# One transformer block in fp32 precision on one core: the values of steps 0 and 1, 2 and 3, 4 and 5, 6 and 7 taken together, the next input's transposes ahead of the last first-layer slice, and the first layer's banks dealt out anew

## The chip, the core and the metric
The kernel runs on one of the eight cores of a Trainium2 chip. The time is that of the device, in microseconds (us). The engines of the core are TensorE (PE, with its weight loads as PEld), VectorE (DVE), ScalarE (ACT), GpSimd (POOL) and SyncE (SP, which issues the DMAs). Each runs its own program in order, and semaphores join them.

## The reference
There are 32 inputs of 512 tokens by 256 features. Each goes through attention and a feed-forward part, both with a residual:
```
x = x + attention(layernorm(x))
x = x + 0.5 * (silu(layernorm'(x) @ w1 + b1) @ w2 + b2)
```
The attention is linear, with 16 heads of 16 features, q and k through elu(x)+1, and causal in chunks of 128 tokens. For each chunk (n = 4 of them) and head:
```
scores = mask(q k^T);  num = scores v + q S;  den = sum(q * (cumsum(k) + z))
out = num / den;  S += k^T v;  z += sum(k)
```
The first layer w1 is 256 by 1024, the second w2 1024 by 256, both dequantised from integers. layernorm' has a gain and an offset.

## The kernel before
The work is a software pipeline over the 32 inputs. One pass of the loop, called a **slice** here, does the attention of input i, the feed-forward part of input i-1 and the projection of q and k of input i+1. Slice 0 has no feed-forward part; slices 1 to 29 are the loop, 30 and 31 are written out with parts left away, and slice 32 has the feed-forward part alone. The order on each engine is written out by hand: `pe_iteration` for PE, `ve_iteration` for DVE, `ac_iteration` for ACT, `po_iteration` for POOL.

The attention of a slice has eight **steps** u = 0..7 (two halves t of the heads, four chunks c). For each step:
- `scores(u)`: PE, 4 matmuls of 128 by 256 into two PSUM banks (L454);
- `mask(u)`: DVE, two multiplications by the causal mask, from the two banks into the buffer `probs[u % 2]` (L624, 128x512 each);
- `values(u)`: PE, 8 matmuls of 32 columns of weights into `num[t]`, 16 records in the trace (L496). It waits for both masks of the step;
- `from_state(u)`: PE, the part from the running state, one matmul, two records (L463); none for chunk 0.

When a head half is done, `attention(t)` on DVE multiplies `num[t]` by the reciprocal denominators (L743). These were transposed by PE in `spread_reciprocals(t)` (L528) and copied by ACT in `reciprocals_out(t)` (L975).

Between the steps PE does the first layer in eight pieces `fc1(j)`, each 4 matmuls of 128x512 into two banks a and b (L390, L391). ACT scales bank a (`ffn_scaled`, L889), DVE adds bank b (`ffn_sum`, L710), ACT takes silu and makes the high part (`ffn_silu`, L897 and L900), POOL makes the low part (L1028). High and low parts exist because every matmul of full precision is made as three.

`x_transposes` (L358) turns the next input over. ACT copies the high part `xt_hi` (L878) and DVE makes the low part `xt_lo` (`input_lo`, L654), one for each half t. `project_kq(0)` and `project_kq(1)` are 12 matmuls of 128x512 each (L328). Then come the second layer `fc2`, the output projection, and, at the slice's end, the values projection, the transposes of the feed-forward input and `scores(0)` of the next slice.

PSUM has 8 banks: `num0`, `num1`, `state_acc`, `sc0`, `sc1` and three of a ring. The table `RING` says which ring bank a use takes, in order of time, and `free_bank` makes a use wait for the last read of the use before it in the same bank. Uses in `BORROWED` take other banks, with waits of their own.

Of the kernel before, what the change touches and what calls it, by code (L numbers as in the profile page):

```python
# [73 lines left out]
def build(nc, x, wq_t, bq, wk_t, bk, wv_t, bv, wo_t, bo, gamma, beta, q1, sc1, b1, q2, sc2, b2, out):  # L74
# [20 lines left out]
    with ExitStack() as ctx:  # L95
# [66 lines left out]
        def by_group(ap):  # L162
# [11 lines left out]
        ring = [bank(f"ring{n}") for n in range(3)]  # L174
        RING = {"ht0": 0, "v1": 2, "kt1": 1, "f1a": 0, "f1b": 2, "f2a": 1, "f2b": 0, "f3a": 2, "f3b": 1, "rb0": 0,
                "f4a": 2, "f4b": 0, "f5a": 1, "f5b": 2, "rb1": 0, "f6a": 1, "f6b": 0, "f7a": 2, "f7b": 1,
                "xt0": 0, "xt1": 2, "k0": 0, "q0": 1, "z0": 0, "wo0": 2, "z1": 1}
        USES = list(RING)
        NEXT_USES = {"xt0", "xt1", "k0", "q0"}

        BORROWED = {"v0": state_acc, "kt0": state_acc, "ht1": num[0], "f0a": num[0], "f0b": num[1], "wo1": num[0]}
        FFN_USES = {"ht0", "ht1", "z0", "z1"} | {f"f{j}{ab}" for j in range(FT) for ab in "ab"}
# [100 lines left out]
        def free_bank(w, use, present):  # L283
# [13 lines left out]
            if use == "f0b":  # L297
                if "rb0" in present:
                    w.need(rden, 0)
                else:  # L300
                    w.need(attn, -1, 1)
                return
            if use == "wo1":
                w.need(attn, 0, 0)
                return
            n = USES.index(use)
# [54 lines left out]
        def pe_iteration(e, i, A, Fn, N, N2, preparation=None, bias_products=None, first=False):  # L361
# [195 lines left out]
            if not A and Fn:  # L557
                fc1(2)
                for j in range(FT):
                    if j + 3 < FT:  # L560
                        fc1(j + 3)
                    fc2_group(j)
                return
            fc1(2)
            if A:
                scores(1)
                update_states()
                values(0)
            for u in range(2, U, 2):
                if u < U - 2:  # L570
                    fc1(2 * (u // 2) + 1)
                if u == U - 2:
                    fc1(FT - 1)
                if A and u < U - 2:
                    spread_reciprocals(u // 2 - 1)
                if A:
                    scores(u)
                if u < U - 2:
                    fc1(2 * (u // 2) + 2)
                elif N:  # L580
                    x_transposes()
                if A:
                    scores(u + 1)
                    values(u - 1)
                    values(u)
                    from_state(u - 1)
                    from_state(u)
            if preparation:
                preparation()
            project_kq(0)  # L590
            if A:
                values(U - 1)
                from_state(U - 1)
            project_kq(1)
# [61 lines left out]
        def ve_iteration(e, i, A, Fn, N, N2, preparation=(None, None, None)):  # L656
# [137 lines left out]
            if A:  # L794
                snapshots(0)
                snapshots(1)
                mask(2)
            ffn_sum(3)
            ffn_sum(4)
            if A:  # L800
                mask(3)
                mask(4)
            ffn_sum(5)
            ffn_sum(6)
            if A:
                mask(5)
                mask(6)
                attention(0)
            ffn_sum(7)
            input_lo()  # L810
            if A:
# [61 lines left out]
        def ac_iteration(e, i, A, Fn, N, N2, preparation=None):  # L873
# [102 lines left out]

            for j in range(3, FT - 1):
                ffn_scaled(j)
                if j in (3, 5):
                    reciprocals_out((j - 3) // 2)  # L980
                ffn_silu(j - 1)
            ffn_scaled(FT - 1)
            if N:
                for t in range(T):
                    w.need(v_pe, 0)
                    transposed_hi(f"xt{t}", t, xt_pe, xt_hi, 1, xt_h)
            def attention_hi(t):
                if A:
# [344 lines left out]
```

How the kernel before makes its waits and increments, by code:

```python
    def need(self, event, shift=0, k=None):  # L63
        k = event.per - 1 if k is None else k
        if self.known.get((id(event), shift), -1) >= k:
            return
        self.known[(id(event), shift)] = k
        value = event.value(self.i + shift, k)
        if not isinstance(value, int) or value > 0:
            self.engine.wait_ge(event.sem, value)
# [1060 lines left out]
        @block.sync  # L1132
        def _(e):
            e.dma_start(x_in[:, :, :], x_v[0]).then_inc(load.sem, 16)
            src = {"q": wq_t, "k": wk_t, "v": wv_t, "o": wo_t}
            for n in WORDER:
                e.dma_start(stage_of(n), src[n].rearrange("(t p) n -> p t n", p=P)).then_inc(p_wdma[n], 16)
            e.dma_start(bias_o[:, :], on_all(bo)).then_inc(p_dma, 16)
            for t in range(T):
                e.dma_start(w1_i[t], q1[t * P:(t + 1) * P, :]).then_inc(p_wdma["1"], 16)
            early(e, store)
            e.wait_ge(p_const, CONSTS - 1)
            e.wait_ge(p_zero, 1)
            sp_iteration(e, -1, False, False, True, True, lambda: e.wait_ge(p_v, V_W1))
            for n in range(2):
# [10 lines left out]
            with e.Fori(1, B - 2) as i:  # L1157
                sp_iteration(e, i, True, True, True, True)
            sp_iteration(e, B - 2, True, True, True, False)
            sp_iteration(e, B - 1, True, True, False, False)
            sp_iteration(e, B, False, True, False, False)
            e.wait_ge(store.sem, store.value(B - 1, 1))
```

## Time and profile before
| | us |
|---|---|
| median of three runs | 1546.86 (1544.33 to 1548.13) |
| the profiled execution, whole | 1547.17 |
| its span in the trace | 1545.3 |
| PE busy | 1500.6 (97%) |
| DVE busy | 1285.4 (83%) |
| ACT busy | 1131.0 (73%) |
| POOL busy | 671.1 (43%) |

PE's matmuls are pipelined: their lengths overlap in the trace. What one costs is therefore read as the distance from its start to the start of the next. The same holds in part for DVE and ACT, where the next instruction starts before the last has ended.

### The profile page before, as it was taken

The page shows a single profiled execution, that of the slowest core. Times are in us where ns is not written, and L with a number is a line of the kernel's source. Part 1 is how long each engine was busy: PE and PEld are TensorE (multiplying, and loading weights), DVE is VectorE, ACT ScalarE, POOL GpSimd, SP SyncE. Part 2 cuts the span into 40 slices and gives each one's busy share as a digit, 9 for nine tenths or more (in the row PEclk, how much of TensorE's full clock was granted, in tenths as well). Part 3 has the DMA queues.
Part 4 walks back from the last instruction along what each step waited for, and adds up shares of the span by engine and source line. Part 5 has one row for each costly group of instructions (what it writes and reads, how often), then busy time and mean ns, then how long its engine had stood idle before and what let it go on. Part 6 is the DMA issues. An engine that isn't in the chain of part 4 may idle for free.

```text
span 1545.3 us, 40671 instructions
## 1 busy us (share of the span) xinstructions
PE 1500.6 (97%) x14820; PEld 1307.8 (85%) x14820; DVE 1285.4 (83%) x2587; ACT 1131.0 (73%) x1917; POOL 671.1 (43%) x466
## 2 busy tenths in 40 slices
PE   5799999999999999999999999999999999999997
PEld 5588888888888888888888888888888888888887
DVE  6888888888888888888888888888888888888865
ACT  4487777787777787777787777787777787777763
POOL 3245344544344544344544344544344444344443
PEclk8899999999999999999999999999999999999999
DMA  7946775555775555775556775556775556765540
GB/s 197 218 104 130 176 175 134 138 126 133 176 176 124 140 131 135 176 176 123 123 145 138 176 163 139 132 130 141 176 166 129 127 138 146 176 173 124 112 97 28
DMA packets 153944, 222.96 MB, mean 144 GB/s; under 512 B 20032, under 2 KB 71488, under 8 KB 153920
## 3 DMA queue, kind: packets, MB, share of 16 engines
q1 hardware_dynamic: 152560, 222.63, 60.6%
q8 instruction: 15, 0.25, 0.1%
q10 hardware_dynamic: 1360, 0.01, 0.1%
q14 instruction: 9, 0.07, 0.0%
HBM read 138.69 MB, written 83.89 MB: 144 GB/s over the span
## 4 chain that ended last, share of the span: by engine, by line
PE 89%; DVE 6%; issue 3%; DMA 1%; ACT 0%; SPq 0%; DVEq 0%; POOL 0%; ACTq 0%
PE ring L328 35%; PE ring L390 7%; PE ring L391 7%; PE num L496 6%; PE sc L454 6%; PE sc L328 5%; PE num L463 3%; PE num L328 3%; PE state_acc L328 3%; PE ring L528 2%; PE state_acc L477 2%; PE state_acc L454 1%; DVE xt_lo L654 1%; DVE qk L743 1%; DVE probs L624 1%
## 5 line engine op out<-in xcount | busy, mean ns | idle before, releaser
L1028 POOL TENSOR_TENSOR s_lo<-silu_f,s_hi 128x512 fp32r<-128x512 f32 x256 | 342.9, 1345 | 498.3 <-ACT s_hi L900 498.2
L624 DVE TENSOR_TENSOR probs<-sc,causal 128x512 f32<-128x512 f32 x416 | 271.5, 685 | 71.8 <-PE sc L454 62.0
L328 PE MATMUL ring<-w_hi,s_hi 128*128 128x256 f32 x992 | 282.7, 285 | 1.8 <-issue 1.8
L328 PE MATMUL ring<-w_lo,s_hi 128*128 128x256 f32 x992 | 279.4, 282 | 0.0
L328 PE MATMUL ring<-w_hi,s_lo 128*128 128x256 f32 x992 | 279.3, 282 | 0.0
L328 PEld LDWEIGHTS ring<-w_hi,s_hi 128*128 128x128 f32 x992 | 187.9, 189 | 15.7 <-issue 14.4
L1044 POOL TENSOR_TENSOR qk<-qk,phi_q 128x512 f32<-128x512 f32 x64 | 82.9, 1296 | 262.6 <-DVE qk L677 262.6
L328 PEld LDWEIGHTS ring<-w_lo,s_hi 128*128 128x128 f32 x992 | 188.2, 190 | 1.3
L328 PEld LDWEIGHTS ring<-w_hi,s_lo 128*128 128x128 f32 x992 | 188.0, 190 | 0.0
L390 PE MATMUL ring<-gt_hi,w_q 128*128 128x512 f32 x441 | 187.4, 425 | 0.0
L889 ACT ACTIVATE silu_f<-ring,bias,scale 128x512 f32<-128x512 f32 x217 | 167.4, 771 | 14.1 <-PE ring L391 11.5
L391 PE MATMUL ring<-gt_lo,w_q 128*128 128x512 f32 x441 | 174.2, 395 | 0.0
L710 DVE SCALAR_TENSOR_TENSOR silu_f<-ring,scale,silu_f 128x512 f32<-128x512 f32 x222 | 165.6, 746 | 10.2 <-ACT silu_f L889 1.4
L1012 ACT ACTIVATE den_rows<-num 128x256 f32<-128x256 f32 x32 | 12.3, 385 | 219.2 <-PE num L511 219.2
L897 ACT ACTIVATE silu_f<-silu_f 128x512 f32<-128x512 f32 x256 | 159.7, 624 | 13.0 <-DVE silu_f L710 9.3
L900 ACT ACTIVATE s_hi<-silu_f 128x512 fp32r<-128x512 f32 x256 | 161.9, 633 | 8.1
L454 PE MATMUL sc<-q_stack,k_stack 96*128 96x256 f32 x832 | 153.8, 298 | 3.5 <-DVE probs L624 2.0
L496 PE MATMUL num<-probs,v_pad 128*32 128x128 f32 x4096 | 145.1, 276 | 1.7 <-DVE probs L624 1.0
L454 PEld LDWEIGHTS sc<-q_stack,k_stack 96*128 96x128 f32 x832 | 121.8, 191 | 19.3 <-DVE probs L624 11.4
L496 PEld LDWEIGHTS num<-probs,v_pad 128*32 128x32 f32 x4096 | 102.7, 110 | 26.6 <-issue 12.3
L390 PEld LDWEIGHTS ring<-gt_hi,w_q 128*128 128x128 f32 x441 | 82.9, 188 | 37.6 <-ACT silu_f L889 11.4
L391 PEld LDWEIGHTS ring<-gt_lo,w_q 128*128 128x128 f32 x441 | 83.4, 189 | 8.8
(189 smaller groups left out, 3816.2 us busy)
## 6 DMA issues: line engine op xcount, KB each, us to landing
k_stack<-k_rows SPq DMA_DIRECT2D x192, 256.0 KB, 4.0
q_stack<-q_rows SPq DMA_DIRECT2D x384, 128.0 KB, 6.3
k_rows<-silu_f SPq DMA_DIRECT2D x128, 256.0 KB, 3.8
q_rows<-probs SPq DMA_DIRECT2D x128, 256.0 KB, 4.1
x_in<-in_x SPq DMA_DIRECT2D x32, 512.0 KB, 8.6
xb<-in_x SPq DMA_DIRECT2D x32, 512.0 KB, 8.3
out<-clip SPq DMA_DIRECT2D x64, 256.0 KB, 7.8
silu_f<-in_q SPq DMA_DIRECT2D x2, 512.0 KB, 10.7
```

Of the source, the lines that this page charges most:

```text
L328: last = e.matmul(target, a, b, start=(n == 0), stop=(n == 3 * len(pairs) - 1))
L390: e.matmul(bank_[:, :], w1_q[:, t, cols], gt_hi[:, t, :], start=True, stop=False)
L391: f_pe.done(e.matmul(bank_[:, :], w1_q[:, t, cols], gt_lo[:, t, :], start=False, stop=True))
L454: last = e.matmul(score_bank(u, r)[:, 2 * n * P:2 * (n + 1) * P], k_stack[:, t, pair, toks], q_stack[:, t, pair, :, toks], start=True, sto ...
L496: last = e.matmul(num[t][32 * pair:32 * pair + 32, c * P:(c + 1) * P], v_pad[:, c, t * HT // 2 + pair, 2 * odd:2 * odd + 2, :], probs[u % ...
L624: masked[r].done(e.tensor_tensor(half_probs(u, r), score_bank(u, r)[:, :].rearrange("p (h q) -> p h q", h=HV), causal[:, None, :].to_broad ...
L710: f_b.done(e.scalar_tensor_tensor(out=slot, in0=ffn_bank(j, 1, A)[:, :], scalar=scale_1[:, 1, j:j + 1], in1=slot, op0=ALU.mult, op1=ALU.add))
L889: f_a.done(e.activation(silu_f[:, j % SLOTS, :], ring_bank(f"f{j}a")[:, :], ACT.Identity, bias=bias_1[:, j:j + 1], scale=scale_1[:, 0, j:j ...
L897: silu.done(e.activation(slot, slot, ACT.Silu))
L900: sh.done(e.activation(s_hi[:, j, :], slot, ACT.Copy))
L1028: sl.done(e.tensor_tensor(s_lo[:, j, :], silu_f[:, j % SLOTS, :], s_hi[:, j, :].bitcast(F32), ALU.subtract))
L1044: qkcum.done(e.tensor_tensor(qk[:, t, :], qk[:, t, :], phi_q[:, t, :], ALU.mult))
```

## The change
On PE, `scores(1)` goes ahead of `fc1(2)`. The values go in pairs (0,1), (2,3), (4,5), (6,7); before they went 0, (1,2), (3,4), (5,6), 7. `x_transposes` goes ahead of `fc1(7)`, and `values(6)` follows `project_kq(0)` together with `values(7)`. On DVE, `mask(3)` goes ahead of `ffn_sum(3)`, `mask(5)` ahead of `ffn_sum(5)`, `attention(0)` stands between `mask(4)` and `mask(5)`, and `input_lo` ahead of `ffn_sum(7)`. On ACT, the copies `xt_hi` go ahead of `ffn_silu(5)` and `ffn_scaled(7)`. The ring's banks are dealt out anew; `f7b` borrows `num0`.

```diff
--- before.py
+++ after.py
@@ -172,13 +172,13 @@
         state_acc = bank("state_acc")
         sc = [bank(f"sc{r}") for r in range(2)]
         ring = [bank(f"ring{n}") for n in range(3)]
-        RING = {"ht0": 0, "v1": 2, "kt1": 1, "f1a": 0, "f1b": 2, "f2a": 1, "f2b": 0, "f3a": 2, "f3b": 1, "rb0": 0,
-                "f4a": 2, "f4b": 0, "f5a": 1, "f5b": 2, "rb1": 0, "f6a": 1, "f6b": 0, "f7a": 2, "f7b": 1,
-                "xt0": 0, "xt1": 2, "k0": 0, "q0": 1, "z0": 0, "wo0": 2, "z1": 1}
+        RING = {"ht0": 0, "v1": 2, "kt1": 1, "f1a": 0, "f1b": 2, "f2a": 1, "f2b": 0, "rb0": 2, "f3a": 1, "f3b": 0,
+                "f4a": 2, "f4b": 1, "rb1": 0, "f5a": 2, "f5b": 1, "f6a": 0, "f6b": 2, "xt0": 1, "xt1": 0, "f7a": 2,
+                "k0": 0, "q0": 1, "z0": 0, "wo0": 2, "z1": 1}
         USES = list(RING)
         NEXT_USES = {"xt0", "xt1", "k0", "q0"}
 
-        BORROWED = {"v0": state_acc, "kt0": state_acc, "ht1": num[0], "f0a": num[0], "f0b": num[1], "wo1": num[0]}
+        BORROWED = {"v0": state_acc, "kt0": state_acc, "ht1": num[0], "f0a": num[0], "f0b": num[1], "f7b": num[0], "wo1": num[0]}
         FFN_USES = {"ht0", "ht1", "z0", "z1"} | {f"f{j}{ab}" for j in range(FT) for ab in "ab"}
 
         SCORES = {(0, 0): 0, (0, 1): 1, (1, 0): 0, (1, 1): 1, (2, 0): 0, (2, 1): 1, (3, 0): 0, (3, 1): 2,
@@ -300,8 +300,13 @@
                 else:
                     w.need(attn, -1, 1)
                 return
+            if use == "f7b":
+                if "rb0" in present:
+                    w.need(attn, 0, 0)
+                return
             if use == "wo1":
                 w.need(attn, 0, 0)
+                w.need(f_b, -1)
                 return
             n = USES.index(use)
             m = n - 1
@@ -561,35 +566,42 @@
                         fc1(j + 3)
                     fc2_group(j)
                 return
+            if A:
+                scores(1)
             fc1(2)
             if A:
-                scores(1)
                 update_states()
                 values(0)
-            for u in range(2, U, 2):
-                if u < U - 2:
-                    fc1(2 * (u // 2) + 1)
-                if u == U - 2:
-                    fc1(FT - 1)
-                if A and u < U - 2:
-                    spread_reciprocals(u // 2 - 1)
+                values(1)
+                spread_reciprocals(0)
+            for u in range(2, U - 2, 2):
                 if A:
                     scores(u)
-                if u < U - 2:
-                    fc1(2 * (u // 2) + 2)
-                elif N:
-                    x_transposes()
+                fc1(u + 1)
                 if A:
                     scores(u + 1)
-                    values(u - 1)
+                fc1(u + 2)
+                if A:
                     values(u)
-                    from_state(u - 1)
-                    from_state(u)
+                    values(u + 1)
+                    for step in range(u - 1 if u == 2 else u, u + 2):
+                        from_state(step)
+                    if u == 2:
+                        spread_reciprocals(1)
+            if A:
+                scores(U - 2)
+            if N:
+                x_transposes()
+            fc1(FT - 1)
+            if A:
+                scores(U - 1)
             if preparation:
                 preparation()
             project_kq(0)
             if A:
+                values(U - 2)
                 values(U - 1)
+                from_state(U - 2)
                 from_state(U - 1)
             project_kq(1)
             if bias_products:
@@ -795,19 +807,19 @@
                 snapshots(0)
                 snapshots(1)
                 mask(2)
+                mask(3)
             ffn_sum(3)
             ffn_sum(4)
             if A:
-                mask(3)
                 mask(4)
+                attention(0)
+                mask(5)
             ffn_sum(5)
             ffn_sum(6)
             if A:
-                mask(5)
                 mask(6)
-                attention(0)
+            input_lo()
             ffn_sum(7)
-            input_lo()
             if A:
                 mask(7)
             if A:
@@ -974,16 +986,21 @@
                     w.need(rb_pe, 0, t)
                     rb_sb.done(e.activation(qk[:, t, :], ring_bank(f"rb{t}")[:, :], ACT.Copy))
 
-            for j in range(3, FT - 1):
-                ffn_scaled(j)
-                if j in (3, 5):
-                    reciprocals_out((j - 3) // 2)
-                ffn_silu(j - 1)
-            ffn_scaled(FT - 1)
+            reciprocals_out(0)
+            ffn_scaled(3)
+            ffn_silu(2)
+            ffn_scaled(4)
+            ffn_silu(3)
+            reciprocals_out(1)
+            ffn_scaled(5)
+            ffn_silu(4)
+            ffn_scaled(6)
             if N:
                 for t in range(T):
                     w.need(v_pe, 0)
                     transposed_hi(f"xt{t}", t, xt_pe, xt_hi, 1, xt_h)
+            ffn_silu(5)
+            ffn_scaled(7)
             def attention_hi(t):
                 if A:
                     w.need(attn, 0, t)
```

In the pieces below, names with a number are PSUM banks or buffers, and the brackets name the semaphores that an instruction waits for. The first is PE's order in the loop at steps 4 and 5, before: scores(5), values(3) with values(4), from_state(3), fc1(6).
```order
L454 MATMUL state_acc<-q_stack,k_stack 128x256 [waits masked1]
L454 MATMUL state_acc<-q_stack,k_stack 128x256
L454 MATMUL sc1<-q_stack,k_stack 128x256 [waits masked0]
L454 MATMUL sc1<-q_stack,k_stack 128x256
L496 MATMUL num0<-probs1,v_pad 32x128 x8
L496 MATMUL num1<-probs0,v_pad 32x128 [waits masked1]
L496 MATMUL num1<-probs0,v_pad 32x128 x7
L463 MATMUL num0<-phi_q,k_tok 128x128
L390 MATMUL ring2<-gt_hi,w1_q 128x512 [waits f_b]
```
The same place of the changed kernel, from the second half of scores(5): fc1(6), values(4) with values(5), from_state(5).
```order
L459 MATMUL sc1<-q_stack,k_stack 128x256 [waits masked0]
L459 MATMUL sc1<-q_stack,k_stack 128x256
L395 MATMUL ring0<-gt_hi,w1_q 128x512 [waits rb_sb]
L396 MATMUL ring0<-gt_lo,w1_q 128x512
L71 REGISTER_ALU
L395 MATMUL ring2<-gt_hi,w1_q 128x512 [waits f_a]
L396 MATMUL ring2<-gt_lo,w1_q 128x512
L501 MATMUL num1<-probs0,v_pad 32x128 [waits masked1]
L501 MATMUL num1<-probs0,v_pad 32x128 x7
L501 MATMUL num1<-probs1,v_pad 32x128 [waits masked1,masked0]
L501 MATMUL num1<-probs1,v_pad 32x128 x7
L468 MATMUL num1<-phi_q,k_tok 128x128
```
Values(5), which reads `probs1`, now follows values(4) directly; before, values(4) was the last there, and values(5) stood behind the scores of steps 6 and 7.

The second is PE's order in the loop ahead of the projection of q and k, before: the second half of the transposes, scores(7), values(5) with values(6), from_state, first matmul of the projection.
```order
L358 MATMUL ring2<-ident,x_hat 128x128 [waits f_a]
L358 MATMUL ring2<-ident,x_hat 128x128 x3
L454 MATMUL sc1<-q_stack,k_stack 128x256 [waits masked1]
L454 MATMUL sc1<-q_stack,k_stack 128x256
L454 MATMUL sc0<-q_stack,k_stack 128x256 [waits masked0]
L454 MATMUL sc0<-q_stack,k_stack 128x256
L496 MATMUL num1<-probs1,v_pad 32x128 x8
L496 MATMUL num1<-probs0,v_pad 32x128 [waits masked1]
L496 MATMUL num1<-probs0,v_pad 32x128 x7
L463 MATMUL num1<-phi_q,k_tok 128x128 x2
L71 ISA
L328 MATMUL ring0<-xt_hi,wk_hi 128x512 [waits xt_l]
```
The same place of the changed kernel: the second half of the transposes, fc1(7), scores(7), first matmul of the projection.
```order
L71 REGISTER_ALU
L363 MATMUL ring0<-ident,x_hat 128x128 [waits f_a]
L363 MATMUL ring0<-ident,x_hat 128x128 x3
L395 MATMUL ring2<-gt_hi,w1_q 128x512 [waits f_b]
L396 MATMUL ring2<-gt_lo,w1_q 128x512
L395 MATMUL num0<-gt_hi,w1_q 128x512 [waits attn]
L396 MATMUL num0<-gt_lo,w1_q 128x512
L459 MATMUL sc1<-q_stack,k_stack 128x256 x2
L459 MATMUL sc0<-q_stack,k_stack 128x256 [waits masked0]
L459 MATMUL sc0<-q_stack,k_stack 128x256
L71 ISA
L333 MATMUL ring0<-xt_hi,wk_hi 128x512 [waits xt_l]
```
Before, the first half of the transposes went to `ring0` and the second to `ring2`; now the first goes to `ring1` (just above the piece) and the second to `ring0`, where the projection of k starts. Values and from_state no longer stand ahead of the projection.

The third is DVE's order in the loop at steps 4 and 5, before.
```order
L624 TENSOR_TENSOR probs0<-sc1,causal 128x512 [waits av_pe,sc_pe]
L624 TENSOR_TENSOR probs0<-sc0,causal 128x512
L71 REGISTER_ALU
L71 REGISTER_ALU [waits f_a]
L710 SCALAR_TENSOR_TENSOR silu_f<-ring2,scale_1,silu_f 128x512 [waits f_pe]
L71 REGISTER_ALU
L71 REGISTER_ALU [waits f_a]
L710 SCALAR_TENSOR_TENSOR silu_f<-ring0,scale_1,silu_f 128x512 [waits f_pe]
L624 TENSOR_TENSOR probs1<-state_acc,causal 128x512 [waits av_pe,sc_pe]
L624 TENSOR_TENSOR probs1<-sc1,causal 128x512
```
The same place of the changed kernel.
```order
L636 TENSOR_TENSOR probs0<-sc1,causal 128x512 [waits av_pe,sc_pe]
L636 TENSOR_TENSOR probs0<-sc0,causal 128x512
L755 TENSOR_TENSOR qk<-num0,qk 128x512 [waits num_pe,rb_sb]
L71 REGISTER_ALU
L636 TENSOR_TENSOR probs1<-state_acc,causal 128x512 [waits av_pe,sc_pe]
L636 TENSOR_TENSOR probs1<-sc1,causal 128x512
L71 REGISTER_ALU [waits f_a]
L722 SCALAR_TENSOR_TENSOR silu_f<-ring1,scale_1,silu_f 128x512 [waits f_pe]
L71 REGISTER_ALU
L71 REGISTER_ALU [waits f_a]
L722 SCALAR_TENSOR_TENSOR silu_f<-ring2,scale_1,silu_f 128x512 [waits f_pe]
```
Between the masks of step 4 and those of step 5 stand two `ffn_sum` (L710) before, and `attention(0)` (L755) now; the two sums follow the masks of step 5.

## Rows read from the trace of the kernel before
**Rows 1.** The page, parts 1 and 2: busy time of the engines, and the granted clock.
```profile
PE 1500.6 (97%) x14820; PEld 1307.8 (85%) x14820; DVE 1285.4 (83%) x2587; ACT 1131.0 (73%) x1917; POOL 671.1 (43%) x466
...
PEclk8899999999999999999999999999999999999999
```

**Rows 2.** Chain of waits, longest pieces: start us, length us, what; second layer.
```profile
108.64 7.12 PE ring L328 x60
...
1455.89 7.12 PE ring L328 x60
```

**Rows 3.** Timeline of PE, one slice: start us, length us, instruction.
```profile
409.86 0.50 PE L390 MATMUL ring<-gt_hi,w_q 128*128 128x512 f32 x1
410.20 0.40 PE L391 MATMUL ring<-gt_lo,w_q 128*128 128x512 f32 x1
...
414.21 0.39 PE L390 MATMUL ring<-gt_hi,w_q 128*128 128x512 f32 x1
...
415.16 0.50 PE L454 MATMUL sc<-q_stack,k_stack 96*128 96x256 f32 x2
...
415.82 1.08 PE L496 MATMUL num<-probs,v_pad 128*32 128x128 f32 x32
416.83 0.71 PE L463 MATMUL num<-phi_q,k_tok 128*128 128x128 f32 x4
417.30 0.48 PE L390 MATMUL ring<-gt_hi,w_q 128*128 128x512 f32 x1
417.62 0.40 PE L391 MATMUL ring<-gt_lo,w_q 128*128 128x512 f32 x1
...
423.01 0.40 PE L454 MATMUL sc<-q_stack,k_stack 96*128 96x256 f32 x2
...
423.49 1.04 PE L358 MATMUL ring<-ident,x_hat 128*128 128x128 f32 x8
424.29 0.72 PE L454 MATMUL sc<-q_stack,k_stack 96*128 96x256 f32 x4
...
425.95 0.71 PE L463 MATMUL num<-phi_q,k_tok 128*128 128x128 f32 x4
426.89 0.50 PE L328 MATMUL ring<-xt_hi,wk_hi 128*128 128x512 f32 x1 [0.23 <-DVE xt_lo L654]
...
429.89 0.64 PE L496 MATMUL num<-probs,v_pad 128*32 128x128 f32 x16
430.46 0.49 PE L463 MATMUL num<-phi_q,k_tok 128*128 128x128 f32 x2
...
433.60 0.28 PE L328 MATMUL ring<-w_hi,s_hi 128*128 128x256 f32 x1
```

**Rows 4.** Timeline of DVE, the same slice; idle time and its releaser in brackets.
```profile
419.43 1.29 DVE L624 TENSOR_TENSOR probs<-sc,causal 128x512 f32<-128x512 f32 x2 [0.98 <-PE sc L454]
...
423.69 0.69 DVE L624 TENSOR_TENSOR probs<-sc,causal 128x512 f32<-128x512 f32 x1 [0.22 <-PE state_acc L454]
424.30 0.68 DVE L624 TENSOR_TENSOR probs<-state_acc,causal 128x512 f32<-128x512 f32 x1
...
426.15 1.28 DVE L654 TENSOR_TENSOR xt_lo<-ring,xt_hi 128x512 fp32r<-128x512 f32 x2
...
431.48 0.75 DVE L666 SCALAR_TENSOR_TENSOR phi_k<-ring,bias_qk,clip 128x512 f32<-128x512 f32 x1 [2.05 <-ACT clip L927]
```

**Rows 5.** Timeline of ACT, the same slice.
```profile
425.69 0.63 ACT L991 ACTIVATE gt_hi<-qk 128x512 fp32r<-128x512 f32 x1 [0.47 <-DVE qk L743]
426.23 0.61 ACT L897 ACTIVATE silu_f<-silu_f 128x512 f32<-128x512 f32 x1
...
427.41 0.62 ACT L897 ACTIVATE silu_f<-silu_f 128x512 f32<-128x512 f32 x1
```

**Rows 6.** Timeline of DVE in slice 0.
```profile
47.16 1.29 DVE L624 TENSOR_TENSOR probs<-sc,causal 128x512 f32<-128x512 f32 x2 [2.07 <-PE sc L454]
```

**Rows 7.** Busy time by stretch, slice 0: PE, PEld, DVE, ACT, POOL, clock, DMA.
```profile
45.00:50.00 5.00, 4.32 (x59) 3.44 (x54) 2.26 (x5) 0.60 (x1) 2.27 (x1) 1.00 1.07 340
```

## The prediction
> **What bounds the kernel now.** I read the page first: PE is busy for 97% of the span, DVE for 83%, ACT for 73%, at full clock but for the first two fortieths [rows 1]. So PE sets the time, and others matter only where PE waits for them. Next the length of a slice: the 60 second-layer matmuls start at 108.64 and, 29 slices later, at 1455.89 [rows 2]; that is 1347.25 / 29 = 46.46 us, and the loop's slices are alike. Then PE's timeline in one slice, start to start. A slice here is PE's work plus four small losses, and the change touches all of them.
>
> Unit costs on PE, each from start to start [rows 3]. Four first-layer matmuls: 414.21 to 415.16, 0.95 us. Four scores matmuls: 423.01 to 423.49, 0.48. The eight transposes: 423.49 to 424.29, 0.80; I add the 0.07 that the last of such matmuls leaves to the next group (as from_state does, below), 0.87. Values of two steps: 415.82 to 416.83, 1.01; of one step: 429.89 to 430.46, 0.57. So a second step joined to a first costs 0.44, and a block of values has 0.13 that it pays once.
>
> Unit costs on DVE and how fast a wait ends [rows 3, 4]. Masks start 0.60 apart (423.69, 424.30) and one lasts 0.68. The last of the four scores matmuls that start at 423.01 starts at 423.37 and lasts 0.28 (the length of the 256-column matmul at 433.60), so it ends at 423.65; its mask starts at 423.69, 0.04 later. The first `xt_lo` starts at 426.15, ends about 0.68 later at 426.83, and PE goes on at 426.89: 0.06 later. And a matmul that waited could not load its weights beforehand: 409.86 to 410.20 is 0.34 where a first-layer matmul takes 0.235, so each wait costs about 0.10 on top.
>
> **The change part by part, for one slice of the loop.**
>
> One block of values less. Before there are five blocks (0 is joined to the state update), now four. A block costs its 0.13; on entry, the four scores from 415.16 take 0.66 to 415.82 where 0.48 is their work and 0.10 the reload after a wait, so 0.08; on leaving, from_state of two steps takes 0.47 (416.83 to 417.30) and the first-layer matmul behind it 0.32 (to 417.62) where 0.235 is its work, so 0.09. Sum 0.30: gain 0.30. Bounds: 0.1 (only the part inside the block) to 0.4.
>
> fc1(2) no longer waits. It waits at 409.86 for ACT's copy of fc1(1)'s bank: about 0.10, and 0.10 reload. `scores(1)`, 0.48, now stands between. Gain 0.20; bounds 0.1 to 0.2.
>
> scores(3) keeps its wait. Its first bank must be masked for step 2, and fc1(3) alone lies between, as before. The 415.16 row is this wait: its two matmuls take 0.34 to the next rather than 0.24. Cost 0, bounds -0.1 to 0.1.
>
> values(3) waits now. It follows values(2), where before it stood a step later. Count from the start of the last scores(3) matmul. DVE: 0.28 + 0.04, one mask start 0.60, one mask 0.68, 0.05 to PE: 1.65. PE: 0.12 + fc1(4) 0.95 + entry 0.08 + values(2) 0.44 = 1.59. Wait 0.06, and about 0.04 for a load of only 32 columns: cost 0.10, bounds 0 to 0.2.
>
> values(5) waits now, and this is the largest new item. From the last scores(4) matmul, DVE does two masks, `attention(0)`, two masks: 0.28 + 0.04 + 4 x 0.60 + 0.68 + 0.05 = 3.45. DVE is free by then: it idles 0.98 ahead of these masks [rows 4], and has less to do there now. PE: 0.12 + fc1(5) 0.95 + scores(5) 0.48 + fc1(6) 0.95 + 0.08 + values(4) 0.44 = 3.02. Wait 0.43, with the load 0.47. Bounds 0.2 to 0.6. Behind the waiting instruction on PE stand scores(6), the transposes and the whole projection, so nothing hides it.
>
> The projection of k. Before: from_state at 425.95 would end its 0.47 at 426.42, and the projection starts at 426.89 [rows 3]; wait 0.47. This is what putting the transposes first should cure. But the second half of the transposes now goes to `ring0`, where the projection of k starts, so that the projection waits for both low parts rather than for one. From the last scores(6) matmul: 0.28 + 0.04, two masks and the first `xt_lo` 3 x 0.60, the second `xt_lo` 0.68, 0.05: 2.85, and the reload 0.10 makes 2.95. PE: 0.12 + transposes 0.87 + fc1(7) 0.95 + scores(7) 0.48 = 2.42. Wait 0.53 against 0.47: cost 0.06. Bounds -0.3 (the first low part were enough, 0.60 earlier, less what comes late elsewhere) to 0.2.
>
> fc2(0) may wait now. It takes `ring0` after `phi_k`. Between `xt_hi` and the exponentials ACT does one silu pair more (426.23 to 427.41, 1.18) and one scaling (about 0.7), and saves the 0.47 idle ahead of 425.69 [rows 5] and a little more: the exponentials come 1.3 later, and with them `phi_k`, which follows ACT directly (2.05 idle ahead of it [rows 4]). From the transposes' start, `phi_k` ended at 431.48 + 0.75 - 423.49 = 8.74, now 10.0. PE came to fc2(0) after 433.60 - 423.49 = 10.11, and now after 0.87 + 0.95 + 0.48 + 0.53 + 2.82 + (0.10 + 1.01 + 0.47 + 0.08) + 2.82 = 10.13. The margin is 0.1, of the size of the reload. I take 0.10, bounds 0 to 0.3.
>
> Per slice: -0.30 - 0.20 + 0.10 + 0.47 + 0.06 + 0.10 = +0.23. I round it to 0.2, since two of the terms are of the size of my reading. Slices 1 to 30: 30 x 0.2 = 6. Slice 31 has no next input: -0.5 + 0.57, about 0.1.
>
> **Slice 0** has no first layer on PE, so DVE and PE wait for each other there. Before, DVE still had the odd step's masks while PE did values; now each pair of steps is closed before the next begins. From the end of mask(3) to the start of mask(4), PE does values(3) 0.44 + 0.13, from_state(1, 2, 3) 0.7, four transposes 0.44, scores(4) 0.48 and some 0.4 of releases and leaving: 2.6; between mask(1) and mask(2) it is some 1.0 behind the state's snapshots, between mask(5) and mask(6) 0.57 + 0.24 + 0.48 + 0.4 = 1.7. DVE's idle time there is 2.07 ahead of 47.16 in the profile [rows 6], with about 1.6 at the other two places by the same counting, and DVE is busy for only 2.26 of the 5 us at 45 to 50 [rows 7]. That makes 5.3 against 3.7, 1.6 more; and the projection now follows mask(6) and both low parts (1.2 + 1.3 behind scores(6)) where it had been reached with them done: 1.4 more. Cost 3; bounds 0 (DMA or DVE hides it later) to 5 (PE is longer at the lower clock, of which the two 8s of [rows 1] tell).
>
> Sum: 6 + 0.1 + 3 = 9.1, against the profiled execution's own 1547.17 (span 1545.3 and 1.9 around it). It lies 0.3 over the median of the runs, within their spread. **Forecast: 1556.3 us.** Its own range by the bounds of the terms that matter: -0.05 to +0.45 a slice and 1 to 5 for slice 0, 1547 to 1566, and mostly 1551 to 1561.
>
> **The rivals.**
>
> *The gains win (faster).* If the wait at values(5) is covered, a slice is -0.24, and the whole 1547.2 - 7.2 + 3 = 1543. Place: PE's arrival at values(5). It decides at 0.23: with a wait there under that, a slice is shorter than before. For it: the gains of 0.30 and 0.20 are read from rows, and if leaving a block costs more than I can see they grow. Against: five DVE instructions of known length stand between scores(4) and values(5), and PE's work between is shorter by 0.4.
>
> *It cancels (no change).* A slice at 0 to +0.05 and slice 0 hidden behind its DMAs and DVE's preparation of the weights: 1547 to 1550. For it: the three small terms (values(3), projection, fc2(0)) sum to 0.26 and each could be nil. Against: slice 0's chain goes through DVE, which has no slack to hide it in.
>
> *ACT becomes late (slower still).* Its chain from the exponentials on is 1.3 later while PE is only 0.2 later. If the denominators or the next slice's inputs have under 1.1 of slack, up to 0.5 a slice more: 1556 + 15 = 1571.
>
> *The clock falls (slower still).* Three waits a slice instead of one large one. The clock stays at full in the loop although each slice has its 0.47 us wait [rows 1], which speaks against it. If PE did 1 us of each slice at 1.2 GHz, it would take 2: 1556 + 31 = 1587. The Trainium skill ("TensorE: Matmul & The Clock Gate", section A second HAM failure mode) says that a kernel whose PE idles briefly and often between groups of matmuls lost throughput to a clock that goes down and up; by that rule this rival would come true, and no row here shows it yet.
>
> **How the numbers follow.** Forecast 0.72, faster rival 0.10, cancelling 0.12, ACT late 0.04, clock 0.02. A measurement of this kernel tells about 0.3% (4.6 us) from no change. Below 1542.2 is faster: half of the faster rival and tails, 0.08. Slower, above 1551.5: nearly all of the forecast's own share and the two slower rivals, 0.76. The rest, 0.16, is no change. Range 1549 to 1563, which leaves out most of the faster rival and the slowest cases.
>
> **What would show it.** The slice by the distance between the second layers: 46.6 to 46.7 rather than 46.46. On PE, values of one step followed by an idle or stretched start (about 0.45) where values(5) starts, released by the mask; four blocks of values; no stretch at fc1(2) in its new place; 0.5 ahead of the projection, released by the second `xt_lo`. In slice 0, DVE idle 2.6 or more ahead of mask(4), and the first second layer 3 us later. It is wrong if the slice is under 46.5, or if PE comes to values(5) with both masks done.

## The result, and the profile after

| | before | after |
|---|---|---|
| time, median of 5 runs each | 1545.0 us | 1581.45 us (1580.27 to 1585.82) |
| ratio | | 1.0242, interval 1.0228 to 1.0256 |
| span of the profiled execution | 1545.3 us | 1578.5 us |
| one slice of the loop | 46.46 us | 47.42 us |

The change costs 2.4%, four times the 9 us that were forecast; 1563 was the end of the range. Two executions among the experiments below, far slower than the others of their kernel (1619.05 and 3652.11 us), count in no median or ratio. The page, parts 1 and 2, as [rows 1] of before:
```profile
PE 1514.8 (96%) x14820; PEld 1302.0 (82%) x14820; DVE 1325.2 (84%) x2587; ACT 1125.2 (71%) x1917; POOL 670.6 (42%) x466
...
PEclk8899999999999999999999999999999999999999
```
The clock is as before. DVE has the same 2587 instructions and is busy for 39.8 us more: some of them last longer, namely two kinds of subtraction that make low parts, `silu_f<-phi_k,silu_f` (70.7 us in all before, 89.2 after) and `gt_lo<-qk,gt_hi` (49.9 and 73.6). The chain of waits gives the slice, as [rows 2]:
```profile
114.35 7.12 PE ring L333 x60
...
1489.41 7.25 PE ring L333 x60
```
(1489.41 - 114.35) / 29 = 47.42. So 0.96 a slice was added, where 0.2 was forecast. The list of waits of after (what PE waited with, its line, the releaser; then us in total, times, longest) says where:
```profile
PE num L501 <- DVE probs L636: 14.2, 34, 1.4
PE ring L333 <- DVE xt_lo L666: 11.6, 32, 2.0
...
PE ring L363 <- ACT x_hat L957: 7.8, 31, 3.0
```
The first is mainly values(5), the second the projection; both were forecast. The third wasn't: in the kernel before PE waited for ACT's `x_hat` once in the whole run, for 2.4 us; now in every slice. `x_hat` (the program's name for the normalised input of the feed-forward, `hn2`) is what the first-layer transposes read at the end of a slice.

PE's timeline of one slice of after. A slice is measured here from its feature transposes (`state_acc<-ident,phi_k`):
```profile
418.99 0.60 PE L438 MATMUL state_acc<-ident,phi_k 128*128 128x128 f32 x4
...
428.55 1.25 PE L501 MATMUL num<-probs,v_pad 128*32 128x128 f32 x32
429.73 0.94 PE L468 MATMUL num<-phi_q,k_tok 128*128 128x128 f32 x6
...
433.85 0.64 PE L501 MATMUL num<-probs,v_pad 128*32 128x128 f32 x16
434.84 0.65 PE L501 MATMUL num<-probs,v_pad 128*32 128x128 f32 x16 [0.35 <-DVE probs L636]
435.41 0.49 PE L468 MATMUL num<-phi_q,k_tok 128*128 128x128 f32 x2
...
438.02 0.64 PE L459 MATMUL sc<-q_stack,k_stack 96*128 96x256 f32 x4
...
438.96 0.50 PE L333 MATMUL ring<-xt_hi,wk_hi 128*128 128x512 f32 x1 [0.29 <-DVE xt_lo L666]
...
446.31 0.34 PE L333 MATMUL ring<-w_hi,s_hi 128*128 128x256 f32 x1
446.50 0.28 PE L333 MATMUL ring<-w_lo,s_hi 128*128 128x256 f32 x1
...
461.38 0.38 PE L525 MATMUL num<-ident,den_rows 128*128 128x128 f32 x2
463.03 0.72 PE L363 MATMUL ring<-ident,x_hat 128*128 128x128 f32 x3
463.91 0.33 PE L363 MATMUL ring<-ident,x_hat 128*128 128x128 f32 x1 [0.16 <-ACT x_hat L957]
464.07 0.60 PE L363 MATMUL num<-ident,x_hat 128*128 128x128 f32 x4
...
466.42 0.60 PE L438 MATMUL state_acc<-ident,phi_k 128*128 128x128 f32 x4
```
The other engines in the same slice of after (ACT, DVE, POOL):
```profile
436.86 1.09 ACT L890 ACTIVATE xt_hi<-ring 128x512 fp32r<-128x512 f32 x2 [2.15 <-PE ring L363]
444.10 0.67 ACT L936 ACTIVATE clip<-ring,bias_qkm 128x512 f32<-128x512 f32 x1
461.77 2.08 ACT L957 ACTIVATE x_hat<-x,hn_add,ln_rstd 128x256 f32<-128x256 f32 x4 [1.31 <-DVE hn_add L874]
441.77 1.64 DVE L666 TENSOR_TENSOR gt_lo<-qk,gt_hi 128x512 fp32r<-128x512 f32 x1
447.39 1.36 DVE L701 TENSOR_TENSOR silu_f<-phi_k,silu_f 128x512 fp32r<-128x512 f32 x1
456.10 0.66 DVE L854 TENSOR_TENSOR x<-ring,xb 128x512 f32<-128x512 f32 x1
439.19 1.30 POOL L1045 TENSOR_TENSOR s_lo<-silu_f,s_hi 128x512 fp32r<-128x512 f32 x1 [3.80 <-ACT s_hi L912]
440.46 2.40 POOL L1052 TENSOR_TENSOR xb<-xb,bias_o 128x1024 f32<-128x1024 f32 x1
442.82 2.99 POOL L1045 TENSOR_TENSOR s_lo<-silu_f,s_hi 128x512 fp32r<-128x512 f32 x2
445.76 2.44 POOL L1056 TENSOR_TENSOR res<-res,bias 128x1024 f32<-128x1024 f32 x1
```
And the rows of before that answer to them, beyond [rows 3 to 5] (the next slice's feature transposes start at 453.00, so this one's at 453.00 - 46.46 = 406.54):
```profile
430.12 0.67 ACT L924 ACTIVATE clip<-ring,bias_qkm 128x512 f32<-128x512 f32 x1
447.60 2.07 ACT L945 ACTIVATE x_hat<-x,hn_add,ln_rstd 128x256 f32<-128x256 f32 x4
433.41 0.68 DVE L689 TENSOR_TENSOR silu_f<-phi_k,silu_f 128x512 fp32r<-128x512 f32 x1
437.97 1.53 DVE L689 TENSOR_TENSOR silu_f<-phi_k,silu_f 128x512 fp32r<-128x512 f32 x1
441.76 0.66 DVE L842 TENSOR_TENSOR x<-ring,xb 128x512 f32<-128x512 f32 x1
430.54 2.41 POOL L1039 TENSOR_TENSOR res<-res,bias 128x1024 f32<-128x1024 f32 x1
437.66 1.29 POOL L1044 TENSOR_TENSOR qk<-qk,phi_q 128x512 f32<-128x512 f32 x1 [4.71 <-DVE qk L677]
448.57 0.38 PE L520 MATMUL num<-ident,den_rows 128*128 128x128 f32 x2
450.22 0.60 PE L358 MATMUL ring<-ident,x_hat 128*128 128x128 f32 x4
450.65 0.60 PE L358 MATMUL num<-ident,x_hat 128*128 128x128 f32 x4
453.00 0.60 PE L433 MATMUL state_acc<-ident,phi_k 128*128 128x128 f32 x4
```
Subtract the slice's start from each and compare:

| from the slice's start, us | before | after | later by |
|---|---|---|---|
| ACT, first exponential (`clip<-ring`) | 23.58 | 25.11 | 1.53 |
| PE, fc2(0) | 27.06 | 27.32 | 0.26 |
| DVE, `x` (the attention's output added) | 35.22 | 37.11 | 1.89 |
| ACT, the four `x_hat`, start | 41.06 | 42.78 | 1.72 |
| PE, transposes of the denominators | 42.03 | 42.39 | 0.36 |
| PE, the transposes of `x_hat` into `num`, behind the wait | 44.11 | 45.08 | 0.97 |

Up to fc2(0) PE is 0.26 later; the forecast had 0.13 ahead of fc2(0) and 0.10 at it. At the denominators it is 0.36 later, where 0.23 was forecast. What follows, 0.97 - 0.36 = 0.61, is the wait for `x_hat`, of which the forecast had nothing. The last `x_hat` of before is ready at 447.60 + 2.07 = 449.67; the fourth transpose needs it some 0.33 behind 450.22, at 450.55. That is 0.88 of slack, the time by which an input is ready before PE reads it. Against PE, `x_hat` came 1.72 - 0.36 = 1.36 later, and PE now waits: its four transposes stretch from 0.43 to 1.04.

### The profile page after: what moved, and what is told of

The parts are those of the page before. It is cut to its first block, busy times and chain, and to the rows that moved or that the text cites. A ratio compares the mean times of both kernels' runs of the same rounds, so it can differ in the third digit from the quotient of the medians.

```text
span 1578.5 us, 40769 instructions
## 1 busy us (share of the span) xinstructions
PE 1514.8 (96%) x14820; PEld 1302.0 (82%) x14820; DVE 1325.2 (84%) x2587; ACT 1125.2 (71%) x1917; POOL 670.6 (42%) x466
## 4 chain that ended last, share of the span: by engine, by line
PE 65%; DVE 23%; issue 6%; ACT 4%; DMA 1%; DVEq 0%; SPq 0%; POOL 0%; ACTq 0%
PE ring L333 24%; PE num L501 8%; DVE probs L636 5%; PE sc L333 5%; PE sc L459 5%; PE num L468 4%; PE ring L395 4%; PE ring L396 4%; ACT x_hat L957 3%; DVE stats L859 3%; DVE stats L645 2%; DVE x L854 2%; DVE xt_lo L666 2%; DVE qk L689 2%; PE ring L533 2%
## 5 line engine op out<-in xcount | busy, mean ns | idle before, releaser
L501 PE MATMUL num<-probs,v_pad 128*32 128x128 f32 x4096 | 154.1, 278 | 14.3 <-DVE probs L636 14.2
L395 PE MATMUL ring<-gt_hi,w_q 128*128 128x512 f32 x410 | 164.9, 402 | 0.0
L396 PE MATMUL ring<-gt_lo,w_q 128*128 128x512 f32 x410 | 161.7, 394 | 0.0
L501 PEld LDWEIGHTS num<-probs,v_pad 128*32 128x32 f32 x4096 | 101.9, 110 | 67.5 <-issue 47.5
L722 DVE SCALAR_TENSOR_TENSOR silu_f<-ring,scale,silu_f 128x512 f32<-128x512 f32 x191 | 137.0, 743 | 5.4
L957 ACT ACTIVATE x_hat<-x,hn_add,ln_rstd 128x256 f32<-128x256 f32 x128 | 66.5, 590 | 56.2 <-DVE hn_add L874 56.2
L701 DVE TENSOR_TENSOR silu_f<-phi_k,silu_f 128x512 fp32r<-128x512 f32 x64 | 89.2, 1394 | 0.0
```

The costliest lines, as they stand in the source:

```text
L395: e.matmul(bank_[:, :], w1_q[:, t, cols], gt_hi[:, t, :], start=True, stop=False)
L396: f_pe.done(e.matmul(bank_[:, :], w1_q[:, t, cols], gt_lo[:, t, :], start=False, stop=True))
L501: last = e.matmul(num[t][32 * pair:32 * pair + 32, c * P:(c + 1) * P], v_pad[:, c, t * HT // 2 + pair, 2 * odd:2 * odd + 2, :], probs[u % ...
L722: f_b.done(e.scalar_tensor_tensor(out=slot, in0=ffn_bank(j, 1, A)[:, :], scalar=scale_1[:, 1, j:j + 1], in1=slot, op0=ALU.mult, op1=ALU.add))
L957: e_hn2.done(e.activation(hn2[:, c, :], x1[:, c, :], ACT.Identity, bias=hn2_add[:, c:c + 1], scale=ln2_rstd[:, 1, c:c + 1]))
```

## The experiments

The theory (A): ACT does the inputs' copies `xt_hi` ahead of the silu of block 5, stands idle for them (2.15 at 436.86), and all its later work in the slice is late by 1.53. In addition GpSimd's add of bias_2 now collides with DVE's subtraction for the low part of phi_k (they overlap in time, and the subtraction lasts 1.36 instead of 0.68). Both run down one chain: exponentials, DVE's features, `x`, statistics, GpSimd's rsqrt, ACT's `x_hat`. Rivals: PE's own new waits are dearer than they look; slice 0; the removed waits come back. Ratios are to the kernel before, run beside it. The slice is taken each time from the second layers in the chain of waits, as above.

**One ACT step back.**
```
 ffn_scaled(6)
+ffn_silu(5)
 if N: ... transposed_hi(...)      # xt_hi
-ffn_silu(5)
 ffn_scaled(7)
```


> The changed kernel, with one pair of ACT moved back: the silu of slice 5 and its high part ahead of the copies of the transposed input, in the time in which ACT idles for the transposes. Theory A (late chain): the changed kernel loses most of its time because ACT reaches the exponentials 1.53 us later in each slice; DVE's features, layer-norm statistics and the normalised input of the feed-forward part follow, and PE waits about 0.75 us for the latter ahead of its transposes at the slice's end. Then this edit takes about 1.2 us off the delay, PE's wait there and the one at the first second-layer matmul go, the slice falls from 47.41 to about 46.6 and the time from 1581 to 1556 (1550 to 1562). Theory B (PE's own waits at values(5), the projection and the pairs were mis-sized, and the late chain is covered): the slice stays over 47.1 and the time over 1572. Theory C (collisions of DVE and POOL alone): the time falls by under 15 us and the 1.35 us subtraction for the low part of k stays.

Measured: 1560.74 us, ratio 1.0096 (1.0073 to 1.0120); slice 46.73. One instruction pair's place on ACT gives back 21 of the 36 us. The wait for `x_hat` falls to 2 times a run, and the subtractions for phi_k's low part are again as before (mean 1104 ns against 1394 in after). What remains, 0.27 a slice, is PE's own part, close to the 0.23 that the prediction had summed for it.

**The add of bias_2 earlier on GpSimd**, ahead of its low part of block 4 (ACT still late).
```
 for j in range(2, FT):
+    if Fn and j == 4: res += bias_2
     ...
     ffn_lo(j)
-if Fn: res += bias_2
```


> The changed kernel, with POOL's addition of the bias to the residual (2.4 us) moved ahead of the fifth low part of the feed-forward, out of the stretch in which DVE subtracts the high part of k. Theory C (a part of the loss is a collision: DVE's first subtraction for the low part of k takes 1.35 us beside this addition, 0.68 in the kernel before): the subtraction falls to 0.7, the features of the second half are no longer 0.33 further behind, PE's wait at the slice's end falls by about 0.33, the time by about 10 us to 1571. Theory A without C: the length of that subtraction does not come from POOL, nothing moves, 1581. Both allow that the addition itself delays POOL's low parts by 2.4 us without anyone waiting.

Measured: 1571.04 us, 1.0161 (1.0137 to 1.0185); slice 47.09. DVE's subtraction lasts 0.69 again, though the exponentials are as late as in after; `x` comes 1.55 later than before, not 1.89. So about 0.33 a slice of the loss (47.42 - 47.09) is the collision. PE still waits for `x_hat`, 14 times in the list (5.0 us): here the lateness alone overruns the slack.

**DVE's attention(0) behind mask(5).**
```
 mask(4)
-attention(0)
 mask(5)
+attention(0)
```


> The changed kernel, with attention(0) on DVE behind mask(5) rather than ahead of it. Forecast by my own term: the wait of PE at values(5) falls from 0.45 to about 0.05, which is about 0.4 a slice. Theory A: the end of the slice is set by the chain through ACT and DVE, which is not a bit shorter except where it starts from PE (the transposes come up to 0.4 earlier, so ACT's copies do too): the time falls by up to 0.35 x 31, to about 1571, if the chain moves with PE, and not at all if ACT is bound by itself. Theory B: it falls by 0.4 x 31 = 12 us or more, to 1569 or less.

Measured: 1568.68 us, 1.0145 (1.0116 to 1.0173); slice 47.04. PE's waits for masks at L501 fall from 14.2 us (34) to 2.6 (3); those for `xt_lo` grow from 11.6 to 14.4; those for `x_hat` stay (7.9). PE comes to the transposes sooner, so ACT's copies and exponentials come 0.38 sooner too, which is what the slice gains. The time lies just within B's range, but the interval (1564 to 1573 us) covers both theories; what speaks for A is that the waits for `x_hat` stay and that the exponentials move by as much as the slice.

**The late ACT step put into the kernel before.** Nothing else is changed.
```
 ffn_scaled(6)
-ffn_silu(5)
 ffn_scaled(7)
 if N: ... transposed_hi(...)      # xt_hi
+ffn_silu(5)
```


> The kernel before, with nothing changed but ACT: the copies of the transposed input ahead of the silu of slice 5 (one pair, 1.2 us of which ACT had idled about half). Theory A: ACT reaches the exponentials about 0.7 us later; the fourth normalised chunk of the feed-forward input had about 0.75 of slack, so that PE waits 0 to 0.3 at the slice's end, more if DVE's subtraction now meets POOL: the time rises by 0 to 10 us. With PE's order untouched every rise is the late chain's. Theory B: no rise.

Measured: 1568.73 us, 1.0150 (1.0128 to 1.0173): +23 us, more than was expected. Slice 47.13. ACT's exponentials are only 0.57 later, but DVE's subtraction and GpSimd's add stand so:
```profile
439.87 2.00 DVE L689 TENSOR_TENSOR silu_f<-phi_k,silu_f 128x512 fp32r<-128x512 f32 x1
...
438.91 2.40 POOL L1041 TENSOR_TENSOR res<-res,bias 128x1024 f32<-128x1024 f32 x1
...
454.89 2.08 ACT L945 ACTIVATE x_hat<-x,hn_add,ln_rstd 128x256 f32<-128x256 f32 x4 [1.36 <-DVE hn_add L862]
```
2.00 where it was 0.68, and the slack of 0.88 is overrun: PE waits for `x_hat` 40 times, 8.7 us. A step moved on ACT reproduces two thirds of the loss with PE's order untouched. Is it the lateness or the collision?

**The same with the add of bias_2 early**, by the second experiment's edit.


> The kernel before with two edits: ACT copies the transposed inputs ahead of the silu of block 5 (the edit of the earlier run that cost 23 us), and GpSimd adds bias_2 to res ahead of its fourth low part instead of behind its last. In that earlier run the exponentials came 0.58 us later in a slice, the subtraction of phi_k's high part lasted 2.00 us instead of 0.68 beside GpSimd's work, and the inputs of the next feed-forward came 1.44 us later for a slack of some 0.8. Theory A (lateness and stretch add up against one slack): with the add gone the subtraction lasts 0.68, the inputs come 0.6 later, which the slack of 0.8 holds, and a slice is 46.5 long: 1545 to 1552. Rival B (ACT's lateness costs by itself, the stretch is a symptom): 30 x 0.5 more than before, 1560 or more. Rival C (the add is harmful wherever it stands, since it takes DVE's time elsewhere): also over 1560, and the phi_k subtraction still above 1 us.

Measured: 1547.4 us, 1.0006 (0.9995 to 1.0017), as A expected. The subtraction:
```profile
437.12 0.68 DVE L689 TENSOR_TENSOR silu_f<-phi_k,silu_f 128x512 fp32r<-128x512 f32 x1
```
The slice is (1456.49 - 111.82) / 29 = 46.37 and PE waits for `x_hat` once. ACT is as late as in the run before and it costs nothing: lateness below the slack is free, the collision on top is what overruns it. A collision has no cost of its own either: DVE's `gt_lo` subtractions are stretched here as in the run before (mean 1391 ns, 780 in the kernel before), and the slice is none the longer for it.

**The banks of the transposed inputs exchanged**, so that the projection needs the first low part alone.
```
-"xt0": 1, "xt1": 0,
+"xt0": 0, "xt1": 1,
```


> The changed kernel with the banks of the two transposed inputs exchanged: the first goes to ring0, where the projection of k starts, so that the projection waits for the first low part alone. Theory A (the end of a slice is set by the chain ACT exponentials, DVE, GpSimd, ACT x_hat, whose start ACT's own queue sets): the 0.5 us wait ahead of the projection goes, but the same time stands as a wait ahead of the second layer and of the next feed-forward's transposes, so nothing is gained: 1576 to 1583. Rival B (PE's own waits add up to the time, as the prediction summed them): 0.5 x 31 = 16 us less, 1563 to 1568.

Measured: 1580.69 us, 1.0222 (1.0207 to 1.0237), slice 47.41: nothing. Waits of PE:
```profile
PE ring L363 <- ACT x_hat L957: 7.8, 31, 2.9
PE ring L333 <- DVE phi_k L678: 5.6, 30, 0.3
```
The waits for `xt_lo` fall from 11.6 us (32) to 1.9 (2), and fc2(0) waits for phi_k instead. While the chain sets the end, curing PE's wait ahead of it moves it.

**Slice 0 alone in the old order on PE.**
```
 update_states(); values(0)
+if not Fn: for u in 2, 4, 6: scores(u); scores(u + 1); values(u - 1); values(u); from_state(u - 1); from_state(u)
+          project_kq(0); values(7); from_state(7); project_kq(1) ...
```


> The changed kernel, but PE goes through slice 0, and only that, in the order of before (values of steps 1 and 2, 3 and 4, 5 and 6 together, the last behind the first projections). It tests the prediction's term of 3 us for slice 0. Theory A: the distance from slice 0's first transposes to slice 1's goes back from 49.9 to about 47 us, and the run is 3 us shorter: 1576 to 1580. Rival B (slice 0 is longer for another reason, such as its low parts or ACT's order): no change, 1580 to 1583.

Measured: 1578.1 us, 1.0209 (1.0194 to 1.0224), 3 us less. Feature transposes of slices 0 and 1, in after and then here:
```profile
36.57 1.06 PE L438 MATMUL state_acc<-ident,phi_k 128*128 128x128 f32 x4
```
```profile
36.97 1.02 PE L438 MATMUL state_acc<-ident,phi_k 128*128 128x128 f32 x4
...
85.19 0.60 PE L438 MATMUL state_acc<-ident,phi_k 128*128 128x128 f32 x4
```
In after slice 1's transposes start at 86.51: 49.94 behind, against 46.64 before (34.80 to 81.44). Here it is 48.22: of the 3.3, 1.7 come back. In this execution PE also waited 1.35 for the DMA of q_stack. One execution says little here, since this distance varies from kernel to kernel by more than that. Over all thirteen profiles it is 46.30 to 48.76 in the six kernels in which PE goes through slice 0 in the old order (before, its three variants, this run and the next), with a mean of 47.2, and 49.05 to 52.44 in the seven with the new order, with a mean of 51.2. The two groups do not overlap, and this run and the next, which share much of their other code with after, lie in the first. So PE's order in slice 0 does cost time, by these means about 4 us.

**All mended**: the edits shown for the ACT step, the banks, attention(0), the early add and slice 0, in one kernel.


> The changed kernel with five edits together: silu of block 5 ahead of ACT's input copies, the transposed inputs' banks exchanged, attention(0) behind mask(5) on DVE, GpSimd's add of bias_2 early, and slice 0 in the old order on PE. Theory A: the chain to the next feed-forward's inputs is in time and the new waits are gone, all but about 0.1 at values(5) and 0.2 at the projection, so that the prediction's gains of 0.5 a slice remain: 1525 to 1540, faster than both kernels. Rival B (the gains of joined steps and of fc1(2) are not real, or something else such as the clock takes them): 1545 to 1560.

Measured: 1531.76 us, ratio 0.9909 (0.9895 to 0.9922): faster than both kernels. The second layers in the chain,
```profile
110.02 7.12 PE ring L333 x60
...
1442.08 7.13 PE ring L333 x60
```
and, in one slice, values(2) with values(3), and the projection behind scores(7):
```profile
414.48 1.25 PE L501 MATMUL num<-probs,v_pad 128*32 128x128 f32 x32
415.66 0.94 PE L468 MATMUL num<-phi_q,k_tok 128*128 128x128 f32 x6
...
423.57 0.64 PE L459 MATMUL sc<-q_stack,k_stack 96*128 96x256 f32 x4
424.09 0.50 PE L333 MATMUL ring<-xt_hi,wk_hi 128*128 128x512 f32 x1
```
PE waits for `x_hat` 4 times, 2.9 us in all. The slice is 45.93, 0.53 under before. That this equals the prediction's two gains (0.30 for a block of values, 0.20 at fc1(2)) is chance, since two other things changed as well. The wait ahead of the projection fell from 0.47 to 424.09 - 423.57 - 0.48 = 0.04, and the pairs of values at 414.48 and at 419.78 still take 1.18 each, 0.17 over their 1.01. With 0.23 for fc1(2) (the last experiment), 0.53 + 2 x 0.17 - 0.43 - 0.23 = 0.21 are left for the block of values. So both gains are there, fc1(2)'s by an experiment of its own, the block's by what is left over, and smaller than the 0.30 that was read.

**The ACT step and the banks**, the two edits shown above together.


> The changed kernel with the silu of block 5 ahead of ACT's input copies (alone 1560.7) and the transposed inputs' banks exchanged (alone worth nothing). Theory A (bank exchange is worth the wait ahead of the projection once the late chain is in time): 0.5 less a slice, 15 us: 1543 to 1548. Rival B (the exchange is worth nothing in any setting, since the projection then waits for its second part or the next unit instead): 1558 to 1562.

Measured: 1543.89 us, 0.9975 (0.9964 to 0.9985); slice 46.16 against 46.73 with the ACT step alone. The same exchange of banks that was worth nothing in after is worth 0.57 a slice here.

**The ACT step and attention(0)**, likewise.


> The changed kernel with the silu of block 5 ahead of ACT's input copies, and DVE's attention(0) behind mask(5). It tests the prediction's largest term, the wait of 0.43 at values(5). Theory A: that wait falls to about 0.1 (less by the 0.6 of attention(0), if PE is not kept waiting elsewhere), but the low parts now start as before while PE reaches the projection 0.4 earlier, so most of it comes back there; a gain of about 0.1 a slice, 3 us: 1555 to 1560. Rival B (the wait at values(5) is paid in full and nothing takes it over): 0.4 x 30 = 12 less, 1547 to 1551.

Measured: 1556.28 us, 1.0047 (1.0034 to 1.0060); slice 46.52, 0.21 less than with the ACT step alone; A had 0.1, B 0.4. PE's waits for masks fall from 14.3 us (34) with the ACT step alone to 3.1 (3), and those for `xt_lo` rise from 11.4 (32) to 17.2 (32): about half of values(5)'s wait is handed on to the projection.

**fc1(2) behind scores(1), alone in the kernel before.**
```
-fc1(2)
 scores(1)
+fc1(2)
 update_states()
```


> The kernel before with one edit: PE does scores(1) ahead of fc1(2), as in the changed kernel. It tests the prediction's gain of 0.20 a slice at fc1(2). Theory A: the wait for ACT's copy is covered and a slice is 46.25 long: 6 us less, 1537 to 1542. Rival B (the wait moves to values(0) or to the masks behind scores(1)): 1544 to 1548.

Measured: 1542.1 us, 0.9962 (0.9950 to 0.9974), 0.38% or 5.9 us less than before (4 to 8 by the interval); A expected 6 less. Slice (1451.86 - 111.14) / 29 = 46.23. This part of the change is a gain by itself.

## Why the prediction was wrong

The direction was right, and PE's own part was of the size that was forecast (0.23 a slice; 0.36 measured at the denominators). The time was 25 us short, because a wait of some 0.6 a slice at the slice's end was not in the sum.

- *fc1(2), -0.20.* 0.23 less a slice when it is done alone. *A block of values, -0.30.* About 0.21, as what is left of the slice with all mended; too large by 0.1, within its bounds. No experiment changed it alone.
- *values(3), +0.10; values(5), +0.47.* 429.73 - 428.55 = 1.18 and 435.41 - 433.85 = 1.56 where a block of two takes 1.01 [rows 3]: 0.17 and 0.55. The wait stands where it was said, released by the mask. Right, 0.15 short together.
- *Projection, +0.06.* The scores' 0.48 behind 438.02 end at 438.50; it starts at 438.96. Wait 0.46 against 0.47 before: no cost, where 0.06 was taken.
- *fc2(0), +0.10.* 0.26 later in front of it and 0.36 behind it, at the denominators: 0.10. Its first matmul takes 0.19 to the next (446.31 to 446.50). Right.
- *Slice 0, +3.* 3.3 in the profile of after, and about 4 between the means of the two orders in all profiles. DVE idles 2.60 and 2.65 ahead of the masks of steps 4 and 6, where 2.6 and 1.7 were counted. The size is right, and PE's order is its cause; how far the single parts of the count hold was not tested. The 1.8 that slice 0's transposes start later (36.57 against 34.80) isn't the change: kernels with the same code there start at 35.06 to 37.43, the latest in a variant of before.
- *The step that failed* is "fc2(0) may wait now", where the lateness of ACT was worked out (1.3; measured 1.53) and then costed at fc2(0) alone. The same text says 0.2 for PE and 1.3 for ACT's chain. It should have been followed to the chain's end, where it cost 0.69 a slice in after, fc2(0)'s 0.10 included (47.42 - 46.73, by the first experiment). The rival "ACT becomes late" named the mechanism ("the next slice's inputs have under 1.1 of slack, up to 0.5 a slice more") and gave it 0.04, without reading the slack, which was in the trace: 0.88 from the rows of `x_hat` and its transposes. Lateness by itself, 1.53 - 0.36 against 0.88, makes 0.3. That is the part the rival had (the second experiment has the lateness without the collision, the first has neither: 47.09 - 46.73 = 0.36). The second part, a further 0.33, was in no rival: DVE and GpSimd locking each other out once their steps shift against each other.
- *The clock.* It stayed at its higher level, 2.4 GHz, from the third fortieth of the span on, with a mean of 0.989 over the whole, although each slice has its waits at values(5), at the projection and for `x_hat`. The Trainium skill's rule that the prediction had cited for the clock rival was not borne out here.

In figures, the 33.2 us by which the spans differ: 1.8 at the start, 3.3 in slice 0, 0.6 in slice 1 up to its second layer (114.35 - 108.64 = 5.7 so far), 27.8 in the 29 slices between the second layers, where 0.2 x 29 = 5.8 was forecast, and -0.3 behind them.

## What to carry to other kernels

When an engine off the critical path becomes late by d, follow its chain to the next place where the bounding engine reads it and compare d with the slack there, which is a subtraction of two rows of the timeline; do this for each engine whose order changes. A wait removed upstream of the real bound returns as another wait: the same edit was worth 0 and 0.57 a slice in two states of this kernel. Look also for pairs of DVE and GpSimd instructions that an altered order brings side by side.

## What the hardware showed beyond expectation

DVE's subtraction of two SBUF operands, started beside a GpSimd tensor operation, ended a fixed time behind GpSimd's end, however early it had started. It looks as if it stood until then, rather than ran slower. Ends by the rows above:

| DVE starts | GpSimd ends | DVE ends | difference |
|---|---|---|---|
| before, 437.97 | 437.66 + 1.29 = 438.95 | 439.50 | 0.55 |
| after, 441.77 | 440.46 + 2.40 = 442.86 | 443.41 | 0.55 |
| after, 447.39 | 445.76 + 2.44 = 448.20 | 448.75 | 0.55 |
| silu of block 5 late in before, 439.87 | 438.91 + 2.40 = 441.31 | 441.87 | 0.56 |

Unhindered it takes 0.68. So its length is what is left of GpSimd's instruction plus 0.55: 0.68 to 2.00 for the same work. GpSimd's next instruction pays too: two low parts in a row take 2.99 (442.82), where one takes 1.30 (439.19). DVE's masks, which read one operand from PSUM, show no such stretch: their mean is 685 ns before and 683 after, and those at 423.69 and 424.30 before take 0.69 and 0.68 [rows 4] although GpSimd's 2.39 long add of bias_o starts at 424.03. The Trainium skill ("SBUF — State Buffer", section SBUF: two separate sides) states it as a rule: a DVE operation with two SBUF inputs and a GpSimd operation that reads SBUF hold the shared port pair for the whole instruction, and the later one blocks. The trace agrees in each of the four cases. The prediction had not weighed it.
